# Batch 0 of an attention and gated-cell kernel: one score block and its exponential ahead of the gates, maxima ahead of the cell's update, projections in pairs

## The reference, cut to what matters

```python
xn = _layernorm(x)                                   # x: (8, 512, 128)
qkv = xn @ W_qkv + b_qkv                             # 16 heads of 64
scores = einsum('nqhd,nkhd->nhqk', q, k)
attention = softmax(scores / sqrt(64), axis=3)
out = einsum('nhql,nlhd->nqhd', attention, v).reshape(n, l, DIM) @ W_out + b_out
def step(c, xt):                                     # over the 8 batches
    ft = sigmoid(xt @ wf.T + c @ uf.T + bf)
    it = sigmoid(xt @ wi.T + c @ ui.T + bi)
    gt = tanh(xt @ wc.T + c @ uc.T + bc)
    return ft * c + it * gt, None
c_final, _ = lax.scan(step, c0, xn)
h = tanh(einsum('tbi,oi->tbo', xn, wo) + c_final @ uo.T + bo)
```

## Time and profile before

| | us |
|---|---|
| median of 3 runs | 852.46 (851.73 to 852.64) |
| profiled execution | 851.62 |
| its span | 849.8 |
| TensorE busy | 829.1 (98%) |
| VectorE busy | 535.2 (63%) |
| ScalarE busy | 451.3 (53%) |
| GpSimd busy | 569.5 (67%) |

### The profile page before, as it was taken

One profiled execution on the slowest core, in us unless ns is written; L12 is line 12 of the kernel. 1 busy time (PEld: TensorE's weight loads), 2 busy tenths in 40 slices (PEclk: granted clock), 3 DMA queues, 4 the chain that ended last, 5 costly groups with the idle time before them and its releaser, 6 DMA issues.

```text
span 849.8 us, 15289 instructions
## 1 busy us (share of the span) xinstructions
PE 829.1 (98%) x5365; PEld 468.4 (55%) x5365; DVE 535.2 (63%) x718; ACT 451.3 (53%) x585; POOL 569.5 (67%) x299
## 2 busy tenths in 40 slices
PE   6999999999999999999999999999999999999997
PEld 4656566555555545556555545556555545556442
DVE  6786766666566746676476747666476647766432
ACT  5657565554555525555555525556455525556440
POOL 4639675277577737777577747776577747777475
PEclk9999999999999999999999999999999999999999
DMA  8000000000000000000000000000000000000000
GB/s 248 2 2 1 26 2 1 3 15 26 2 15 14 1 26 13 1 13 26 1 14 14 1 25 13 1 13 26 1 14 13 1 25 13 1 15 2 2 27 12
DMA packets 30028, 14.23 MB, mean 17 GB/s; under 512 B 13202, under 2 KB 27568, under 8 KB 30000
## 3 DMA queue, kind: packets, MB, share of 16 engines
q1 hardware_dynamic: 29952, 13.84, 5.7%
q10 hardware_dynamic: 48, 0.02, 0.0%
HBM read 6.83 MB, written 2.10 MB: 11 GB/s over the span
## 4 chain that ended last, share of the span: by engine, by line
PE 91%; POOL 3%; ACT 2%; DVE 2%; DMA 1%; issue 1%; SPq 0%; POOLq 0%; DVEq 0%
PE st L867 20%; PE misc L881 13%; PE pv L881 13%; PE st L805 10%; PE mx L853 8%; PE st L873 6%; PE mx L907 6%; PE st L900 3%; PE pv L805 2%; PE misc L788 2%; PE misc L805 2%; PE pv L788 1%; ACT probs L424 1%; PE mx L788 1%; POOL PSUMK L313 1%; DMA probs<-in_L_attn_W_qkv_dram 1%
## 5 line engine op out<-in xcount | busy, mean ns | idle before, releaser
L595 DVE TENSOR_REDUCE NM<-mx 128x2 f32<-128x1024 f32 x256 | 313.9, 1226 | 169.1 <-PE mx L853 168.8
L424 ACT ACTIVATE probs<-st 128x1024 f32<-128x1024 f32 x256 | 256.9, 1027 | 70.7 <-PE st L873 63.5
L307 POOL TENSOR_TENSOR PSUMK<-probs 128x1024 f32<-128x1024 f32 x64 | 153.7, 2401 | 179.0 <-ACT probs L424 179.0
L313 POOL TENSOR_TENSOR PSUMK<-PSUMK,probs 128x1024 f32<-128x1024 f32 x64 | 153.1, 2391 | 6.1
L320 POOL TENSOR_TENSOR PSUMK<-PSUMK,probs 128x1024 f32<-128x1024 f32 x64 | 152.8, 2388 | 6.1
L881 PE MATMUL misc<-probs,VALL 128*64 128x512 f32 x512 | 122.1, 598 | 0.0
L881 PE MATMUL pv<-probs,VALL 128*64 128x512 f32 x512 | 117.1, 599 | 0.5 <-DVE RES L565 0.4
L853 PE MATMUL mx<-KH,QH 64*128 64x512 f32 x512 | 106.5, 411 | 2.6 <-DVE NM L595 2.2
L867 PE MATMUL st<-QH,KH 64*128 64x512 f32 x512 | 105.0, 405 | 0.9 <-ACT probs L424 0.9
L867 PE MATMUL st<-QH,KL 64*128 64x512 f32 x512 | 101.3, 390 | 0.0
L873 PE MATMUL st<-MROW,ONEROW 64*128 64x512 f32 x512 | 101.1, 390 | 0.0
(11 more groups left out here) (178 smaller groups left out, 1201.9 us busy)
## 6 DMA issues: line engine op xcount, KB each, us to landing
MROW<-TT SPq DMA_DIRECT2D x256, 1.0 KB
XSH<-XH SPq DMA_DIRECT2D x8, 256.0 KB, 2.4
XSL<-XL SPq DMA_DIRECT2D x8, 256.0 KB, 2.4
RES<-in_L_attn_data_dram SPq DMA_DIRECT2D x8, 256.0 KB, 2.9
out_dram<-RES SPq DMA_DIRECT2D x8, 256.0 KB, 2.3
RX<-R SPq DMA_DIRECT2D x112, 2.0 KB, 1.7
probs<-in_L_attn_W_qkv_dram SPq DMA_DIRECT2D x3, 512.0 KB, 6.0
AT<-in_L_attn_data_dram SPq DMA_DIRECT2D x2, 512.0 KB, 7.2
```

The source lines that it names most:

```text
L307: nc.gpsimd.tensor_tensor(PSUMK[:, s % 2, :, :], e[:, :, 0, :], e[:, :, 1, :], ALU.add).then_inc(sum_part, 1)
L313: nc.gpsimd.tensor_tensor(PSUMK[:, s % 2, :, :], PSUMK[:, s % 2, :, :], probs[:, s % 2, :, 2, :], ALU.add).then_inc(sum_part, 1)
L424: nc.scalar.activation(probs[:, s % 2, :, u, :], st[:, u % 2, :, :], ACT.Exp, scale=SCALE).then_inc(exp_done, 1)
L595: nc.vector.tensor_reduce(NM[:, s % 2, 0:2 * TB].rearrange("p (h b) -> p h b", h=2)[:, :, b], mx[:, :, :], AX.X, ALU.max, negate=True).the ...
```

## The change

In batch 0, on TensorE: in stretch 0 the projections of pair 3 go ahead of the first values; score block (1, 0) goes ahead of the gates; maxima (2, 2, 2) and then gate 1 come right behind gate 0, ahead of `turn_x` and gate 2; the gates wait for five evacuated value banks first and for the sixth ahead of gate 1. In the later stretches block 0 of tile t + 1 goes ahead of the gates, and maxima (t + 3, 0) go from between blocks 0 and 1 into the middle of block 1. The portions of three projection slots are no longer cut: between them stand two or three maxima (stretch 0 holds three, since its scores now hold one less). On ScalarE the exponential of block 0 goes ahead of the tanhs, whose order in stretch 0 becomes 0, 1, 2 by the gates' numbers in the code's list. On VectorE, in stretches 1 to 3, the first maxima of t + 3 go ahead of `admit` and `update`. In stretch 0 maxima (2, 2, 2) go ahead of `forget`, (2, 2, 3) ahead of `admit`, (3, 3, 0) between `admit` and `update`; the moments of batch 4 are cut in two and those of batch 6 move as a whole behind the second update. GpSimd's and SyncE's programs stay as they are.

```diff
@@ -365,10 +365,10 @@
                 act.wait_ge(ld_W[i], 16)
                 nc.scalar.copy(WH[:, i * DIM:(i + 1) * DIM], W_raw[:, i * DIM:(i + 1) * DIM]).then_inc(wh_done, 1)
 
-            def tanh_gate(s, k):
+            def tanh_gate(s, k, place):
 
                 g = GATES[k]
-                act.wait_ge(gate_done, 3 * s + k + 1)
+                act.wait_ge(gate_done, 3 * s + place + 1)
                 nc.scalar.activation(tg if g == 2 else gate_banks[k], gate_banks[k], ACT.Tanh,
                                      bias=bcol[:, B_C:B_C + 1] if g == 2 else bhalf[:, g:g + 1],
                                      scale=1.0 if g == 2 else 0.5).then_inc(t_done, 1)
@@ -458,11 +458,14 @@
                     evac_v(6 + t, 1 if j < 2 else 0, 2 * (j % 2) + k, value_banks[k])
 
             def recur(s):
-                tanh_gate(s, 0)
+                tanh_gate(s, 0, 0)
+                if s == 0:
+                    tanh_gate(s, 2, 1)
                 if s + 1 < N:
                     hi_x(s + 1)
-                tanh_gate(s, 1)
-                tanh_gate(s, 2)
+                tanh_gate(s, 1, 2 if s == 0 else 1)
+                if s > 0:
+                    tanh_gate(s, 2, 2)
 
             def step(n, first, last):
                 for j in range(STRETCHES):
@@ -486,8 +489,9 @@
                         evac_values(t, j)
                         act.wait_ge(gw_lo, 2)
                     if first:
+                        exps(t + 1, s + 1, 0)
                         recur(s)
-                    for u in range(TB):
+                    for u in range(1 if first else 0, TB):
                         exps(t + 1, s + 1, u)
                     if first:
                         keep_state(s)
@@ -684,31 +688,37 @@
                     if first and j == 0:
                         maxima(2, 2, 0)
                         lo_q(3, 3, first_q[3])
+                        lo_k(3, 3, first_k[3])
                         maxima(2, 2, 1)
-                        lo_k(3, 3, first_k[3])
                         moments(3)
+                        maxima(2, 2, 2)
                     elif coming:
                         for b in range(TB):
                             maxima(t + 2, s + 2, b)
                         turn_max(n, t + 2, s + 2)
                     if first:
                         forget(s)
+                        if j == 0:
+                            spread(4)
                         lo_x(s + 1)
-                        if j == 0:
-                            moments(4)
-                        admit(s)
-                        update(s)
                     if first and j == 0:
-                        maxima(2, 2, 2)
+                        aggregate(4)
                         spread(5, (0, 1))
                         maxima(2, 2, 3)
                         turn_max(0, 2, 2)
+                        admit(0)
+                        maxima(3, 3, 0)
+                        update(0)
+                        maxima(3, 3, 1)
                         spread(5, (2, 3))
-                        maxima(3, 3, 0)
+                        maxima(3, 3, 2)
                         aggregate(5)
-                        maxima(3, 3, 1)
-                        spread(6, (0, 1))
-                        maxima(3, 3, 2)
+                    elif first:
+                        maxima(t + 3, s + 3, 0)
+                        admit(s)
+                        update(s)
+                        for b in range(1, TB - 1):
+                            maxima(t + 3, s + 3, b)
                     elif coming:
                         for b in range(TB - 1):
                             if b == 2 and not ahead:
@@ -738,8 +748,7 @@
                     if first:
                         update(s + 1)
                         if j == 0:
-                            spread(6, (2, 3))
-                            aggregate(6)
+                            moments(6)
                         lo_state(s + 2)
                     if first and j < 3:
                         divisors(t, s, mx[:, 1, :], t + 1)
@@ -962,15 +971,20 @@
             pe.wait_ge(pads_set, 4)
             pe.wait_ge(d_xs, 32)
 
-            def gates(s, evacuated):
+            def gates(s, evacuated, between=None):
 
                 pe.wait_ge(xl_done, s + 1)
                 recurrence(0, s, gate_done, s, gate_banks[0])
+                if between:
+                    score_maxima(*between)
+                    pe.wait_ge(v_evac, 6)
+                    recurrence(1, s, gate_done, s, gate_banks[2])
                 pe.wait_ge(red_done, evacuated)
                 if s + 1 < N:
                     turn_x(s + 1)
                 recurrence(2, s, gate_done, s, gate_banks[1])
-                recurrence(1, s, gate_done, s, gate_banks[2])
+                if not between:
+                    recurrence(1, s, gate_done, s, gate_banks[2])
 
             def step(n, first, last):
                 for j in range(STRETCHES):
@@ -1000,29 +1014,28 @@
                         scores(0, 0, 0, 2)
                         scores(0, 0, 0, 3)
                         score_maxima(2, 2, 0)
+                        pe.wait_ge(exp_done, 3)
+                        project(0, 3, 0, q_done, first_q[3])
+                        project(0, 3, DIM, k_done, first_k[3])
                         pe.wait_ge(q_lo, 3)
                         pe.wait_ge(k_lo, 3)
                         project_values(0, 0, (0, 1, 2), 64)
-                        pe.wait_ge(exp_done, 3)
-                        project(0, 3, 0, q_done, first_q[3])
-                        project(0, 3, DIM, k_done, first_k[3])
                         score_maxima(2, 2, 1)
                         project_values(0, 0, (3, 4, 5), 0)
-                        pe.wait_ge(v_evac, 6)
-                        pe.wait_ge(gw_lo, 2)
-                        gates(0, 10)
                         pe.wait_ge(q_lo, 4)
                         pe.wait_ge(k_lo, 4)
                         scores(0, 1, 1, 0)
-                        pe.wait_ge(t_done, 2)
+                        pe.wait_ge(gw_lo, 2)
+                        pe.wait_ge(v_evac, 5)
+                        gates(0, 11, (2, 2, 2))
+                        scores(0, 1, 1, 1)
+                        pe.wait_ge(t_done, 3)
                         pe.wait_ge(xl_done, 2)
-                        score_maxima(2, 2, 2)
-                        scores(0, 1, 1, 1)
                         score_maxima(2, 2, 3)
                         scores(0, 1, 1, 2)
+                        scores(0, 1, 1, 3, (0, 1))
                         score_maxima(3, 3, 0)
-                        scores(0, 1, 1, 3)
-                        score_maxima(3, 3, 1)
+                        scores(0, 1, 1, 3, (2, 3))
                     elif coming:
                         if first:
                             wait(pe, den_used, t)
@@ -1047,13 +1060,14 @@
                         scores(n, t, s, 3, (0, 1))
                         score_maxima(t + 2, s + 2, 3)
                         scores(n, t, s, 3, (2, 3))
+                        scores(n, t + 1, s + 1, 0)
                         pe.wait_ge(v_evac, 6 + t)
                         gates(s, 4 * (t + 3))
-                        scores(n, t + 1, s + 1, 0)
+                        scores(n, t + 1, s + 1, 1, (0, 1))
                         pe.wait_ge(t_done, 3 * s + 2)
                         pe.wait_ge(xl_done, s + 2)
                         score_maxima(t + 3, s + 3, 0)
-                        scores(n, t + 1, s + 1, 1)
+                        scores(n, t + 1, s + 1, 1, (2, 3))
                         scores(n, t + 1, s + 1, 2)
                         scores(n, t + 1, s + 1, 3, (0, 1))
                         score_maxima(t + 3, s + 3, 1)
@@ -1088,18 +1102,23 @@
                         scores(n, t + 1, s + 1, 3)
                         if coming:
                             score_maxima(t + 3, s + 3, 1)
-                    if ahead:
+                    if first:
                         project_pair(s + 4, 0, t, (0, 1, 2))
-                        if not first:
-                            project_values(t, j, (4, 5), 0)
+                        score_maxima(t + 3, s + 3, 1 if j == 0 else 2)
+                        project_pair(s + 5, 1, t, (0, 1, 2))
+                        project_pair(s + 4, 0, t, (3, 4, 5))
+                        score_maxima(t + 3, s + 3, 2 if j == 0 else 3)
+                        project_pair(s + 5, 1, t, (3, 4, 5))
+                        if j == 0:
+                            score_maxima(t + 3, s + 3, 3)
+                    elif ahead:
+                        project_pair(s + 4, 0, t, (0, 1, 2))
+                        project_values(t, j, (4, 5), 0)
                         project_pair(s + 5, 1, t, (0, 1))
-                    if coming and ahead:
                         score_maxima(t + 3, s + 3, 2)
-                    if ahead:
                         project_pair(s + 5, 1, t, (2,))
```

(1 more changed line is left out.)

## The result

The changed kernel takes 848.88 us (median of 5, 848.48 to 849.47) against 852.46 for the one before (median of 5, 851.73 to 853.24): a ratio of 0.9961, 95% interval 0.9949 to 0.9972. Forecast were 849.3 and a range of 847.9 to 851.3. The profiled execution took 848.48, its span 846.6, 3.2 us shorter than before.

What follows compares the result with a forecast made beforehand. TensorE, busy 829.1 of 849.8 us, bounds the kernel, so only its idle time in batch 0 can be won. Gains of 2.0 + 2 x 0.42 + 0.34 = 3.2 us take 852.46 to 849.3; range 847.9 to 851.3.

Steps and rivals of the forecast that it cites:

- Projections first, cost 0: Stretch 0, before the gates: q3, k3 ahead of the first values cost and gain 0, but ready KL of pair 3 earlier.
- The block ahead of the gates: Stretch 0: score block (1,0), 0.92, fills 33.70 to 34.62, where TensorE idled up to 35.06; gates start at 34.71.
- Maxima between the gates, two switches for 0.42: Stretch 0: maxima (2,2,2) between gates add two switches, 2 x 0.21, on TensorE; gate 1 covers the wait for their reduction.
- full drain: If changing the tiling mode drained TensorE, the two switches would cost 0.56 instead of 0.42, the forecast 0.14 later.
- Round trips of 1.8: From one block of maxima on TensorE through VectorE's reduction to the next takes 0.54, 1.23 and 0.05 to 0.14: 1.8 us.
- Forget, lo_state: Later stretches: values stop waiting for forget; in stretch 3 the next values wait for lo_state instead, leaving 0.34 gain.
- A: Half is handed back: VectorE's lateness at maxima in the projections passes to TensorE; gain 1.2 to 1.6, 851.1; chance 0.19.
- D: The moved exponential's waits hold ScalarE and the tanhs behind it; only stretch 0 gains, 850.5; chance 0.05.
- B: Slower: update between reductions 0 and 1 holds reduction 1 back by x in four stretches, 3.2 - 4x; chance 0.04.
- C: More: waits in the projections of stretch 0 and later ones shrink; gain 4.4 us, 848.1; chance 0.10.
- The bounds of the sum: Total gain 0.8 to 4.6: stretch 0 from 1.0 to 2.6, a later stretch from -0.1 to 0.7.

Runs made afterwards that it cites:

- e8: Changed kernel with projections q3, k3 behind the first half of the values again in stretch 0: distance 0.63 longer than the changed kernel, median 850.04 us.
- e11: Kernel before with only projections q3, k3 first, score block (1,0) ahead of the gates and its exponential ahead of the tanhs, in stretch 0: ratio 1.0012.
- e1: Changed kernel with the old order in stretches 1 to 3, so stretch 0 alone is changed: distance 1.86 shorter than the kernel before, median 850.57 us.
- e6: Changed kernel with the gates of step 0 whole, behind the sixth evacuation, and maxima (2,2,2) behind them: distance 0.61 longer, 850.34 us (one execution).
- e7: Changed kernel with an unread VectorE reduction added between update and reduction 1 in stretches 1 to 3: distance 3.42 longer, 854.22 us (one execution).
- e9: Changed kernel, stretches 1 to 3: maxima 1 ahead of block 3, reduced between admit and update; second projection portion ahead of the second pair: 846.79 us.
- e4: Changed kernel with VectorE's admit and update ahead of maxima 0 again in stretches 1 to 3: distance 1.16 longer, median 850.72 us.

## Why the prediction was right

Its main numbers, each from the anchor or from the start of its stretch:

| step | predicted | measured |
|---|---|---|
| gates of step 0, from the anchor | 4.64 | 4.78 |
| gates of step 1, from the anchor | 18.90 | 19.03 |
| stretch 0 gains, at the values | 2.0 | 1.88 |
| lost to the exponential of block 1, stretch 1 | 0.35 | 0.36 |
| lost to reductions 1 and 2, stretch 1 | 0.34, 0.11 | 0.34, 0.07 |
| lost to the three reductions in the projections of stretch 0 | 0.50, 0.11, 0.80 | 0.42, 0.11, 0.79 |
| gates of the next step, gain in stretch 1 | 0.34 | 0.38 |
| stretches 1, 2, 3 gain | 0.42, 0.42, 0.34 | 0.43, 0.43, 0.32 |
| sum | 3.2 | 3.06 |

*Projections first, cost 0.* Mis-sized: the second half of the values, now only one slot behind the first, restarts (32.88 to 33.22, 0.34; why it does so there is not shown), so the gates come 0.14 later from the anchor than worked out. That is the size of the whole difference of the sum (3.18 unrounded, against 3.06). KL was in time, and e8 shows what a late one costs: 0.63.

*The block ahead of the gates.* Right in its place, but the text let it look like a gain of its own. e11 shows it is none alone, since the wait moves to (2,2,3). What makes it pay is argued: e1, which brings the maxima forward as well, gains 1.86.

*Maxima between the gates, two switches for 0.42.* The extra between 35.97 and 37.06 is 0.40 over three slots (1.09 for 0.69), as priced from the earlier trace rows, not the 0.56 of a full drain. What it wins was not separated by e6; that it pays is argued.

*Round trips of 1.8.* Right (1.82 to 1.84 where TensorE waits), and e7 gives the one-for-one slope.

*Forget, lo_state.* Right: values no longer wait for forget, and in stretch 3 lo_state takes over (0.47 idle at 158.06).

The rivals: A did not happen, since reduction 1 started when worked out (78.41, 15.71 behind the start of stretch 1; worked out were 80.48 and 15.75 against the old start at 64.73) and stretch 0 gave 1.88, not 1.2. D did not, since the exponential held nothing back (34.87) and the later stretches gained. B's condition was not met. C did not happen either: the waits stood at about the size worked out; that they can be won is what e9 shows. The bounds of the sum, 0.8 to 4.6, are 0.1 off from the terms given for them (1.0 - 0.3 and 2.6 + 2.1), which changes nothing.

Medians moved 3.6, more than 3.06: the rest must lie outside the distance, in the start, or in clock falls of the kernel before. How it divides between these was not measured. For that reason the median lies 0.4 below the forecast while the gain by distance is 0.12 short of it; the distance is the test of the working.

Two things stay untested. In the later stretches e4 shows TensorE's and ScalarE's part without VectorE's order, but no run has VectorE's order without them. In stretch 0 no run has the maxima between the gates alone.

## What to carry to other kernels

Follow one wait to where it goes before counting it: filling an idle gap ahead of an operation that a slower chain releases again only lengthens the next wait. Where two engines hand one buffer to and fro, count their round trips and put other work, on both engines, where the other one is working; the order on the second engine was worth 1.16 here over three stretches, nearly all that they gained. Of the moves on the first engine that were taken back, the dearest cost 0.63, in one stretch. Compare short gains by a distance between two marks in the trace, not by the whole time, when the start alone varies by 2 us as here.

## What was not expected of the hardware

The clock of a nearly full TensorE can fall in the middle of a kernel. Behind one idle piece of 1.99 us (and one of 0.49) it fell in 10 of 10 executions, behind 1.06 and 0.48 in about one in five (12 of 61; these have a third pause, of 1.19, ahead of the gates, which in e11 is 0.27), and in none of the 51 executions of kernels whose profiles show no pause above 0.63 between 30 and 60 us. Slots took 0.43 instead of 0.23 until the clock came back. A pause of 1.28 in each later stretch of e7 (one execution) was followed by none. e11 ran on one chip, where the kernel before fell in 2 of 13. In the first microseconds slots took 0.43 as well, while the view of the granted clock read 1.00. That the pause in stretch 0 is the cause is argued from these groups; no run varied it alone, and what else must come together stays open.
